# The last stage of a two-layer language-model tower: output projection with its weights stationary, token halves kept apart, square roots on GpSimd

## What is computed

```python
    # h: residual stream, x = _layernorm(h)
    out = u * out @ o_w.T + o_b                     # D1 = 192 channels -> 64
    x_r = silu(_srms((x - out) @ t_w.T + t_b, D1))  # _srms: v / (norm(v) * D1**-0.5 + 1e-8)
    h = h + (x + x_r)
    h = h + _layernorm(h) @ weight.T + bias         # result, (2, 1024, 64)
```

## Time and profile before

| what | us |
|---|---|
| median of 3 runs | 366.43 |
| the runs | 366.21, 366.43, 367.53 |
| the profiled execution, its own time | 368.89 |
| its span, first to last instruction | 367.2 |
| PE busy in the span | 321.1 (87%) |
| DVE busy | 238.5 (65%) |
| ACT busy | 144.5 (39%) |
| POOL busy | 101.6 (28%) |

### The profile page before, as it was taken

How to read it: one execution, slowest core, us unless ns; L and a number is a source line. 1 busy time by engine, 2 the same in 40 slices (tenths; PEclk the granted TensorE clock), 3 DMA queues, 4 the chain that set the end, 5 groups by cost and what they waited for, 6 DMA issues and landing times.

```text
span 367.2 us, 4594 instructions
## 1 busy us (share of the span) xinstructions
PE 321.1 (87%) x1685; PEld 181.8 (50%) x1698; DVE 238.5 (65%) x403; ACT 144.5 (39%) x239; POOL 101.6 (28%) x138
## 2 busy tenths in 40 slices
PE   1329878979989999989999999998999999899995
PEld 0105655633433444647754555555555555467734
DVE  1576898989989641365785555553856677745385
ACT  2013525541666677421554455543450120012260
POOL 5740100470661223100002322221004878700000
PEclk9999999999999999988799999999999999999998
DMA  7939500086000000000000000000000000000001
GB/s 257 317 103 420 220 2 0 11 138 112 2 2 1 3 3 0 2 0 2 0 1 2 0 1 2 0 0 2 1 2 0 0 2 0 0 0 3 0 0 57
DMA packets 6269, 15.29 MB, mean 42 GB/s; under 512 B 1384, under 2 KB 3816, under 8 KB 5608
## 3 DMA queue, kind: packets, MB, share of 16 engines
q1 hardware_dynamic: 5685, 14.48, 12.9%
q0 software_dynamic: 512, 0.53, 0.7%
q10 hardware_dynamic: 51, 0.01, 0.0%
HBM read 12.08 MB, written 0.52 MB: 34 GB/s over the span
## 4 chain that ended last, share of the span: by engine, by line
PE 66%; DVE 17%; ACT 5%; POOL 5%; issue 4%; DMA 2%; SPq 1%; DVEq 0%; POOLq 0%; ACTq 0%
PE ps L301 64%; DVE rw L1472 2%; DVE share L1312 1%; PE ps L530 1%; DMA arena<-arena 1%; DMA idt<-ident 1%; DVE xc L1276 1%; DVE st L1275 1%; DVE arena L1452 1%; PE ps L945 1%; DVE st L1268 1%; POOL share L516 1%; POOL share L517 1%; DVE share L1442 1%; ACT sq L1007 1%
## 5 line engine op out<-in xcount | busy, mean ns | idle before, releaser
L1472 DVE TENSOR_REDUCE rw<-ps 128x1 f32<-128x512 f32 (+2 forms) x80 | 45.7, 628 | 6.1 <-PE ps L301 5.6
L1136 ACT ACTIVATE arena<-ps 128x1024 f32<-128x1024 f32 (+3 forms) x48 | 37.6, 812 | 28.8 <-PE ps L301 28.4
L301 PE MATMUL ps<-bfc_s 128*128 128x512 bf16 (+2 forms) x189 | 46.1, 353 | 0.4 <-issue 0.2
L301 PE MATMUL ps<-arena 96*128 96x512 bf16 (+7 forms) x192 | 42.9, 328 | 3.0 <-DVE rw L1472 1.8
L301 PE MATMUL ps<-xs,e_hi 128*128 128x512 f32 x96 | 41.1, 428 | 0.0
L1541 DVE TENSOR_TENSOR arena<-ps,arena 128x512 f32<-128x512 f32 x48 | 33.0, 691 | 11.2 <-ACT arena L1162 10.8
L1162 ACT ACTIVATE arena<-ps 128x512 f32<-128x512 f32 x48 | 28.7, 598 | 26.1 <-PE ps L301 21.8
L301 PE MATMUL ps<-xs,e_lo 128*128 128x512 f32 x96 | 38.8, 405 | 0.0
L301 PE MATMUL ps<-share,tu_s 128*128 128x384 f32 x96 | 32.5, 488 | 0.0
L301 PEld LDWEIGHTS ps<-arena 96*128 96x128 bf16 (+1 forms) x192 | 15.8, 98 | 30.5 <-DVE rw L1472 14.7
L301 PEld LDWEIGHTS ps<-bfc_s 128*128 128x128 bf16 x196 | 19.6, 101 | 16.8 <-issue 1.9
(11 more groups left out here) (244 smaller groups left out, 491.3 us busy)
## 6 DMA issues: line engine op xcount, KB each, us to landing
arena<-arena SPq DMA_DIRECT2D x24, 96.0 KB, 2.8
w<-wpack SPq DMA_DIRECT2D x1, 2152.5 KB
arena<-tm SPq DMA_DIRECT2D x2, 1024.0 KB, 5.9
arena<-epack SPq DMA_DIRECT2D x1, 1540.0 KB, 11.1
arena<-rope SPq DMA_DIRECT2D x1, 1024.0 KB
tu_s<-tu SPq DMA_DIRECT2D x2, 512.0 KB, 12.0
tk_s<-tk SPq DMA_DIRECT2D x2, 512.0 KB, 13.5
rp<-rpack SPq DMA_DIRECT2D x1, 678.5 KB
```

Of the source, the lines that this page charges most:

```text
L301: return nc.tensor.matmul(o, l, r, start=start, stop=stop, **kw)
L1136: nc.scalar.activation(pt[:, n % PT_SLOTS, :, lo:512], ps[:, bank:bank + 2, lo:512], ACT.Exp, scale=HD ** -0.5).then_inc(S("exp_done"), 1)
L1472: V.tensor_reduce(top_view(m, part)[:, at:at + len(heads), i], src, AXX, ALU.max, negate=True).then_inc(S("ring_read"), 1)
```

## The change

It does four things.

1. The output projection holds the weights `o3` stationary and moves two tiles of `yT3` at a time, so its result comes out transposed. `output_projection(blk, k)` handles two tiles, 3 matmuls with 256 moving columns. The subtraction from x happens in transposed form (`residual`), with `xT` of the layer norm before, which is still there, and writes `tmp`, which is the stationary operand of the next projection. The transposes, their two copies and `xc` = x - o_b are gone. The reversed copies of odd tiles become straight copies; `residual` writes reversed.
2. From there on each half has its own semaphores and its own instructions to the end.
3. The roots of the `_srms` norm move from ACT to POOL, as a power of 0.5 with a tile `halves` of constants, 8 elements in each partition for each half; two ACT table loads (one before the four units) go.
4. The last layer norm's scale is applied after the projection with `w4`, to its result, since the scale is one number for each token. The bias is added by POOL into `x1`, and the sum of half 0 is on POOL, that of half 1 on DVE.

The core of the diff, the new functions and their order:

```diff
-            def output_projection(blk):
-                pe.wait_ge(S("yT3"), 2 * NU * (blk + 1))
-                pe.wait_ge(S("uv_silu"), 2 * NT)
-                for jj in range(4):
-                    n = 2 * (2 * blk + jj - 2) if jj >= 2 else 2 * (2 * blk + 1 - jj) + 1
-                    for c in range(3):
-                        ins = mm(ps[:, 6 + blk, jj * P:(jj + 1) * P], yT3[:, n, c, :], W("o3", c * P, (c + 1) * P),
-                                 start=(c == 0), stop=(c == 2))
+            def output_projection(blk, k):
+                n = 4 * blk + 2 * k
+                pe.wait_ge(S("yT3"), n + 2)
+                for c in range(3):
+                    ins = mm(ps[:, 6 + blk, 2 * k * P:2 * k * P + 2 * P], W("o3", c * P, (c + 1) * P), yT3[:, n:n + 2, c, :],
+                             start=(c == 0), stop=(c == 2))
                 ins.then_inc(S("o3"), 1)
+            def residual_projection(a):
+                pe.wait_ge(S("d3"), 2 * (a + 1))
+                for j in range(4):
+                    ins = mm(ps[:, a, j * P:(j + 1) * P], tmp[:, (4 * a + j) * P:(4 * a + j + 1) * P], W("t3"))
+                ins.then_inc(S("t3"), 1)
+            def last_projection(a):
+                pe.wait_ge(S("h_centred"), a + 1)
+                for j in range(4):
+                    ins = nc.tensor.transpose(ps[:, 2 + a, j * P:(j + 1) * P], xc[:, 4 * a + j].rearrange("p b c -> p (b c)"), idt[:])
+                ins.then_inc(S("T4"), 1)
+                pe.wait_ge(S("xT4"), a + 1)
+                for j in range(4 * a, 4 * a + 4):
+                    ins = mm(ps[:, 4 + a, (j % 4) * P:(j % 4 + 1) * P], xT[:, j * P:(j + 1) * P], W("w4"))
+                ins.then_inc(S("o4"), 1)
...
-            keep_warm(46, 7)
+            keep_warm(24, 7)
+            last_projection(0)
+            keep_warm(4, 7)
+            last_projection(1)
...
+            for a in range(2):
+                pool.wait_ge(S("t3_mean"), a + 1)
+                nc.gpsimd.tensor_tensor(st[:, 3, 8 * a:8 * a + 8], st[:, 1, 8 * a:8 * a + 8], halves[:], ALU.pow).then_inc(S("t3_root"), 1)
+            for a in range(2):
+                pool.wait_ge(S("h_new"), a + 1)
+                nc.gpsimd.tensor_tensor(rows(x1, a), rows(h, a), spread(W("b4"), 1, 4), ALU.add).then_inc(S("h_biased"), 1)
+            nc.gpsimd.tensor_tensor(rows(sq, 0), rows(xc, 0), rows(x1, 0), ALU.add).then_inc(S("final0"), 1)
...
+            for a in range(2):
+                act.wait_ge(S("t3_scaled"), a + 1)
+                nc.scalar.activation(part(xc, a), part(xc, a), ACT.Silu).then_inc(S("t3_silu"), 1)
             next_function(ACT.Sqrt)
+            for a in range(2):
+                act.wait_ge(S("h_centred"), a + 1)
+                nc.scalar.activation(part(sq, a), part(xc, a), ACT.Square).then_inc(S("h_squared"), 1)
+                act.wait_ge(S("T4"), a + 1)
+                nc.scalar.copy(xT[:, 512 * a:512 * a + 512], ps[:, 2 + a]).then_inc(S("xT4"), 1)
+            for a in range(2):
+                act.wait_ge(S("h_var"), a + 1)
+                nc.scalar.activation(st[:, 3, 8 * a:8 * a + 8], st[:, 2, 8 * a:8 * a + 8], ACT.Sqrt).then_inc(S("h_std"), 1)
...
+            residual(0)
+            branch_sum(0)
+            residual(1)
+            branch_squares(0)
+            branch_sum(1)
+            branch_squares(1)
+            branch_scale(0)
+            add_branch(0)
+            branch_scale(1)
+            centre_last(0)
+            add_branch(1)
+            centre_last(1)
+            last_variance(0)
+            last_variance(1)
+            last_scale(0)
+            last_scale(1)
```

More of the change, by code:

```diff
@@ L273, in build @@
         unused = sb("unused", [1, 16])
+        halves = sb("halves", [P, 8])
         wst = sb("wst", [P, N], BF16)
@@ L399, in _ @@
             nc.gpsimd.memset(geo[:, 0, :, R:R + 1], 2.0).then_inc(S("constants"), 1)
+            nc.gpsimd.memset(halves[:], 0.5).then_inc(S("halves"), 1)
             nc.gpsimd.memset(va1[:, :, P:P + 1], 1.0).then_inc(S("constants"), 1)
@@ L1187, in y_columns @@
                 src = ps[:, 4 + n % 2, 0:384].rearrange("p (c t) -> p c t", c=3)
-                nc.scalar.copy(yT3[:, n], src[:, :, ::-1] if n % 2 else src).then_inc(S("yT3"), 1)
+                nc.scalar.copy(yT3[:, n], src).then_inc(S("yT3"), 1)
             for n in range(2 * NT):
@@ L1206, in _ @@
                 y_columns(n)
[L1207 to L1211, removed]
-            for a in range(2):
-                act.wait_ge(S("e3"), a + 1)
-                v = xc[:, 4 * a:4 * a + 4]
-                nc.scalar.activation(v, v, ACT.Silu).then_inc(S("xr"), 1)
-            next_function(ACT.Sqrt)
[L1218 to L1221, removed]
+            part = lambda t, a: t[:, 4 * a:4 * a + 4]
+            for a in range(2):
+                act.wait_ge(S("t3_sum"), a + 1)
+                nc.scalar.activation(part(sq, a), part(xc, a), ACT.Square).then_inc(S("t3_squared"), 1)
+            for a in range(2):
+                act.wait_ge(S("t3_scaled"), a + 1)
+                nc.scalar.activation(part(xc, a), part(xc, a), ACT.Silu).then_inc(S("t3_silu"), 1)
+            next_function(ACT.Sqrt)
+            for a in range(2):
[6 more added lines that the diff above has]
+                nc.scalar.activation(st[:, 3, 8 * a:8 * a + 8], st[:, 2, 8 * a:8 * a + 8], ACT.Sqrt).then_inc(S("h_std"), 1)
         @block.vector
@@ L1645, in _, with residual @@
                 V.tensor_tensor(y3[:, 1], y3[:, 1], us[:, at + NU], ALU.mult).then_inc(S("y3"), 1)
[L1646 to L1650, removed]
+            def residual(a):
+                lo, mid, hi = 512 * a, 512 * a + 2 * P, 512 * a + 4 * P
+                tiles = lambda v: v.rearrange("p (k t) -> p k t", t=P)
+                o3 = tiles(ps[:, 6 + a])
+                dve.wait_ge(S("o3"), 2 * (a + 1))
+                V.scalar_tensor_tensor(out=tiles(tmp[:, lo:mid][:, ::-1]), in0=tiles(xT[:, lo:mid]), scalar=W("ob"),
+                                       in1=o3[:, 1::2], op0=ALU.subtract, op1=ALU.subtract).then_inc(S("d3"), 1)
+                V.scalar_tensor_tensor(out=tiles(tmp[:, mid:hi]), in0=tiles(xT[:, mid:hi]), scalar=W("ob"),
+                                       in1=o3[:, 0::2], op0=ALU.subtract, op1=ALU.subtract).then_inc(S("d3"), 1)
@@ L1651, in _, with branch_sum @@
+            def branch_sum(a):
                 dve.wait_ge(S("t3"), a + 1)
                 V.tensor_tensor(halfj(xc, a), ps[:, a].rearrange("p (j x) -> p j x", j=4), spread(W("tb"), 1, 4),
[L1653 to L1658, removed]
@@ L1659, in _ @@
-            scale_rows(xc, xc, 4, S("e3"))
-            def add_branch(a):
[L1662 to L1671, removed]
```

58 lines of the change are left out of this document (42 added, 16 removed).

## The result

| | before | after |
|---|---|---|
| median of 20 runs, us | 366.96 | 365.71 |
| lowest and highest, us | 365.07, 369.04 | 363.57, 367.53 |
| profiled execution: own time, us | 368.89 | 366.29 |
| its span, us | 367.2 | 364.6 |
| mean granted clock | 0.981 | 0.976 |

The ratio after to before is 0.9952, with a 95% interval of 0.9930 to 0.9974, so the kernel is a little faster, by 0.3 to 0.7%. The forecast was 365.0 us against a median of 366.43, and a span of 364.75.

What follows compares the result with a forecast made beforehand. Bound by PE's order up to 347 us, then by serial steps of 0.6 to 0.7 us. Span 363.75 plus 1.0 for clock made 364.75; 1.4 of 2.4 us counted against the median gave 365.0, range 363.3 to 366.9.

Steps and rivals of the forecast that it cites:

- Output projection, 2.0 us less: Last stage, output projection to second projection's result: bias of half 1 starts at 345.4 instead of 347.38, 2.0 us less.
- Norm by halves, 0.7 us more: Norm and Silu: without the removed load and with scaling by halves, DVE adds half 0 to `h` 0.7 us earlier.
- GpSimd's bias holds off the scaling of half 1: After the Silu of half 0: DVE's scaling of half 1 waits for POOL's bias addition of 1.29 us; 0.85 us lost.
- The last exclusion of the sum: End of the last stage: DVE's last addition waits for POOL's addition of half 0 to 360.6 us, done at 361.3.
- The power at 0.5 us: First norm's roots on GpSimd: a power of 8 elements taken at 0.5 us, with no row to price it.
- eight elements are near the first: For the power: 8 elements lie near the 0.2 us POOL addition of 8, not the 2.4 us of 1048.
- the prediction's two signs of being wrong: Wrong if powers exceed 1 us, or the 256-column output projection from `yT3` in two pieces exceeds 0.45 us per matmul.
- all over 0.4 us counts: If half 1's power holds off half 0's scaling, its time beyond 0.4 us is lost; 2.4 us costs 2.0.
- the second rival: Gain given back: power takes 1 to 2.4 us or clock stays low to the end; 365.8 to 367.3, chance 0.21.
- ACT's order: Behind half 1's Silu: table load 1.28 and dummy 0.25, then squares and copy to 355.15; last roots behind the second copy.
- The clock, 1.0 us: PE's idle gaps make the clock fall from 352 to 356 us on; cost 0.6 to 1.5, taken as 1.0.
- Against the median: Median before read as free of the clock loss: 1.4 of the span's 2.4 us counted, giving 365.0 us.

Runs made afterwards that it cites:

- The filled kernel: Kernel after with `keep_warm` 34 for 24 ahead of half 0 and 5 more before its projection: last stage 45.9 us, median 363.72, ratio 0.9911 to before.
- the filled kernel before: Kernel before with 54 in place of 46 matmuls of `keep_warm`: last stage 48.8 us, median 366.28, ratio 0.9962 to the kernel before.

## Why the forecast came out, step by step

- **Output projection, 2.0 us less.** Right: 48.8 us for the kernel before without its fall, 46.7 for this part alone. Counted to the bias of half 1 it is 2.1 as well, 27.9 us after `tk_s` for 30.0. This is most of what the change brings.
- **Norm by halves, 0.7 us more.** Right in direction and mechanism: the Silu of half 0 starts without a load, and `h` of half 0 is added 31.7 us after `tk_s`, against 34.6 before, 2.9 less where 2.7 was forecast (with the 2.0).
- **GpSimd's bias holds off the scaling of half 1.** The mechanism was right. The size was 0.67 us and not 0.85, because the addition with the bias takes 1.09 us and not 1.29 as in the earlier trace rows. That it also meets the centring of half 1 (0.96 for 0.69) was not foreseen; on this path PE was late anyway. The rule of the Trainium skill (SBUF — State Buffer, Who interferes with whom) holds for the additions: DVE instructions with two SBUF inputs waited for nearly all of the rest of POOL's. It doesn't hold for the power, which reads SBUF too: the scaling beside it kept 0.69 us. By the rule, read literally, the scaling of half 0 would have started at 348.79, and by my estimate the span would be up to 1.4 us longer. A tensor_scalar of 8 elements waited for an addition too. The last exclusion of the sum, DVE's last addition behind POOL's, came as forecast, 0.92 us for 0.69.
- **The power at 0.5 us.** Wrong in size: 1.66. The step that failed is "eight elements are near the first", which took an addition's time as nearest. With it one of the prediction's two signs of being wrong came true, powers longer than 1 us; the other didn't, the matmuls with 256 columns took 0.43 us each. By the prediction's own rule, "all over 0.4 us counts", a power of 1.64 us would have cost 1.2 us and led to the second rival, 365.8 to 367.3. It cost nothing, since half 1's root, done at 348.79, is asked for at 349.42 at the earliest, and since the power didn't hold off the scaling. So two errors cancel here: the power is 1.2 us longer than taken, and the exclusion feared for it isn't there. That the forecast survives its own sign is luck in this place.
- **ACT's order.** Right: load, squares and copy follow without a gap, and the last roots wait behind the second copy. The sum has a slip: 1.28 and 0.25 behind 352.6 make 354.1 and not 354.0. The load with its dummy took 1.40 up to the squares, so 354.0 was the better number.
- **The clock, 1.0 us.** The fall came where it was forecast, from 354.1 us, and 3.4 us long. It cost 1.6 (47.5 against 45.9 with the gaps filled), a little beyond the bound of 1.5. At full clock the forecast span was 363.75. The filled kernel, set to the start of before, ends at 363.3 (362.3 + 317.40 - 316.38): 0.4 less, of which 0.2 are the shorter addition; the rest isn't traced. The two errors nearly cancel: set to the same start, the kernel after ends at 364.9, beside 364.75.
- **Against the median: wrong reason.** "I read the third as one with this loss and the median as one without" was refuted by the filled kernel before: the fall is in the median too. Without that deduction the forecast would have been 366.43 - 2.4 = 364.0. The measured medians differ by only 1.25 and 0.9 us, although the stage is 2.3 shorter in both profiles. So 365.0 is near 365.71 by luck: the wrong deduction took back 1.0 us, and about 1 us of the stage's gain doesn't show in the medians. Why it doesn't stays open, inside the stage or ahead of it, since the stage is known from one execution of each kernel in a batch. A longer low clock in the stage of other executions is one candidate: of the 32 executions of the kernel after, only 7 have the mean clock of the two profiles, 0.976; 21 lie lower, at 0.968 to 0.974, and 4 at 0.985 with a median of 364.0. With the roots on ACT, where the profile had the low clock to the end, 10 of 12 have 0.973. Ahead of the stage, in both profiles of the kernel after the first early fall is 6.8 us long, in those of before 3.4, but the stage starts no later for it (317.09 and 316.72, against 317.40 and, with 54 of `keep_warm`, 316.78). Among the profiles of all kernels its start varies by 2.7 us.

So by the profiles the gain of 2.3 us in the stage is made up as follows: 2.1 from the output projection, 0.8 from the rest at full clock (46.7 to 45.9), and 0.6 back to a larger loss of clock. The 0.8 are a balance: the roots on GpSimd give 0.6, the bias on GpSimd takes 0.67, and the halves and the late scale give what is left, about 0.9, which is a subtraction and no measurement.

Open is also why the clock fell in the profile of the kernel before and not in that of the output projection alone, with a gap of the same 1.9 us. The other seven executions of the latter have the same mean of 0.985 or 0.986, which fits but doesn't show it for them, since a third of those of the kernel before have 0.986 too. I can't move the gap against the rest of PE's work without changing something else, and didn't try.

## What to carry to other kernels

A change that shortens a chain by halves also changes how long TensorE stands still in it: count its idle time afterwards and set the filler matmuls anew, but none ahead of work that waits for the engine. An elementwise operation put on GpSimd costs what it holds off on VectorE, and moving it in time can move that wait to the next instruction with two SBUF inputs, so look at what will lie beside it. Compare stages from one marker to the end before comparing whole executions, since the part in front varied here by more than the change is worth.

## What the hardware showed that I had not expected

- A power on GpSimd took 1.64 us for 8 elements of a partition and 10.77 for 64, about 0.16 us for each further element; an addition of 8 took 0.20.
- It left VectorE alone: additions and a scaling with two SBUF inputs kept 0.55 and 0.69 us in it, while a GpSimd addition held the scaling off to 1.36.
- A tensor_scalar of 8 elements on VectorE waited 0.46 us for a GpSimd addition (0.63 for 0.17).
- The same idle time of 1.9 us on TensorE was followed by a fall of the clock in one kernel and not in another; and after idle times of 2.5 and 1.2 us the low clock lasted 3.4 us in two profiles of one kernel, while in three kernels that differ from it by a few instructions, with idle times of 2.5 to 3.1 and 1.2 us, it lasted to the end (13.0 to 14.8 us).
